# A state-space mixer with a routed expert layer: x projected once, lag tables multiplied on TensorE, powers from coarse and fine factors

## The reference

```python
xz = jnp.einsum('bld,ed->bel', hidden_states, W_in)
x, z = jnp.split(xz, 2, axis=1)
xp = jnp.pad(x, ((0, 0), (0, 0), (w - 1, 0)))          # w = 4 taps, one filter per channel
x = lax.conv_general_dilated(xp, conv_w[:, None, :], (1,), 'VALID', ...)
x = jax.nn.silu(x + conv_b[None, :, None])
# the state-space kernel: dt = exp(log_dt), A = -exp(log_A_real) + i A_imag
# Ct = (C_re + i C_im) * (exp(dt A) - 1) / A
k = 2.0 * jnp.einsum('hn,hnl->hl', Ct, jnp.exp(dtA[:, :, None] * t)).real
y = causal_convolution(x, k)                           # by FFT in the reference
y = (y + x * D[None, :, None]) * jax.nn.silu(z)
mixed = jnp.einsum('bhl,dh->bld', y, W_out)
x = layernorm(hidden_states + mixed)
# each token goes to the one of 8 experts with the largest logit
y = relu(x @ w1[e] + b1[e]) @ w2[e] + b2[e]
out = layernorm(x + y)
```

## Time and profile before

| what | value |
|---|---|
| measured time, median of 3 (range) | 266.92 us (265.96 to 268.56) |
| profiled execution: span | 263.8 us |
| TensorE, matmuls busy | 239.2 us (91%) |
| TensorE, weight loads busy (beside the matmuls) | 215.1 us (82%) |
| VectorE busy | 177.0 us (67%) |
| ScalarE busy | 187.1 us (71%) |
| GpSimd busy | 139.8 us (53%) |
| moved by DMA | 52.06 MB, 197 GB/s on average |
| instructions | 8892 |

### The profile page before, as it was taken

The page is one execution under the profiler, slowest core; times in us unless marked ns, Lnnn a source line. Parts: engine busy times, 40 slices in busy tenths (PEclk is TensorE's granted clock), DMA queues, the critical chain, the costliest instruction groups (busy, mean ns, idle before and its releaser), DMA issues.

```text
span 263.8 us, 8892 instructions
## 1 busy us (share of the span) xinstructions
PE 239.2 (91%) x2763; PEld 215.1 (82%) x2764; DVE 177.0 (67%) x552; ACT 187.1 (71%) x528; POOL 139.8 (53%) x208
## 2 busy tenths in 40 slices
PE   8999979999999899999979999359989999999970
PEld 4888768888887678888869999349979999899960
DVE  1889995997218657777724878842877676566672
ACT  2999999856998778888655665207667777667740
POOL 6000000400009989999624687878746656657545
PEclk9999999999999999999999999759999999999995
DMA  7697884600399999999293221647865676677600
GB/s 232 180 313 288 346 334 150 244 0 0 105 310 332 310 279 296 308 320 302 66 361 120 93 93 41 212 92 191 220 179 172 200 210 164 203 195 208 189 34 6
DMA packets 54267, 52.06 MB, mean 197 GB/s; under 512 B 4415, under 2 KB 42817, under 8 KB 54114
## 3 DMA queue, kind: packets, MB, share of 16 engines
q1 hardware_dynamic: 51506, 46.65, 59.2%
q0 software_dynamic: 2304, 4.34, 4.6%
q10 hardware_dynamic: 432, 0.79, 0.8%
HBM read 38.14 MB, written 14.07 MB: 198 GB/s over the span
## 4 chain that ended last, share of the span: by engine, by line
PE 59%; DVE 10%; ACT 10%; POOL 9%; issue 6%; DMA 5%; SPq 1%; DVEq 0%; ACTq 0%; POOLq 0%
PE banks L1292 13%; PE banks L1477 9%; PE banks L1487 8%; PE banks L1370 7%; POOL dispatched_rows L568 5%; ACT BR L672 5%; PE banks L1380 5%; PE banks L1384 4%; PE banks L1275 3%; PE banks L1357 3%; PE banks L1435 2%; DMA X<-dispatched_rows 2%; POOL RE L558 1%; DMA out<-X 1%; POOL out L576 1%
## 5 line engine op out<-in xcount | busy, mean ns | idle before, releaser
L515 POOL TENSOR_TENSOR Wx<-BR,RE 128x384 f32 (+1 forms) x32 | 47.9, 1548 | 27.9 <-PE banks L1292 26.6
L1292 PE MATMUL banks<-Wx,XT 128*128 128x256 f32 x256 | 59.9, 380 | 1.7 <-ACT Z L643 1.7
L809 ACT ACTIVATE Z<-banks,BR 128x128 f32<-128x128 f32 x156 | 44.6, 368 | 18.4 <-PE banks L1477 18.3
L1292 PEld LDWEIGHTS banks<-Wx,XT 128*128 128x128 f32 x256 | 48.4, 190 | 9.0 <-issue 2.2
L576 POOL DMA_INDIRECT out<-X x39 | 38.4, 986 | 27.8 <-DVE X L1233 15.3
L1477 PE MATMUL banks<-Z 128*128 128x128 f32 x312 | 42.7, 281 | 0.4 <-ACT Z L798 0.2
L1487 PE MATMUL banks<-BR,Z 128*128 x312 | 41.1, 276 | 1.2 <-DVE X L1216 1.2
L1477 PEld LDWEIGHTS banks<-Z 128*128 128x128 f32 x312 | 39.0, 196 | 1.0 <-issue 0.5
L1487 PEld LDWEIGHTS banks<-BR,Z 128*128 128x128 f32 x312 | 37.8, 192 | 1.5 <-issue 1.5
L568 POOL DMA_INDIRECT dispatched_rows<-TR,CR x32 | 31.0, 970 | 9.3 <-POOL RE L558 9.3
L1057 DVE TENSOR_TENSOR X<-banks,Z 128x256 f32 (+1 forms) x32 | 20.4, 636 | 9.1 <-PE banks L1384 9.1
(11 more groups left out here) (220 smaller groups left out, 469.6 us busy)
## 6 DMA issues: line engine op xcount, KB each, us to landing
TR<-kernel_rows SPq DMA_DIRECT2D x32, 512.0 KB, 6.5
Z<-w SPq DMA_DIRECT2D x39, 256.0 KB, 3.1
dispatched_rows<-TR SPq DMA_DIRECT2D x3, 2310.0 KB, 8.8
X<-dispatched_rows SPq DMA_DIRECT2D x39, 66.0 KB, 2.1
XT<-hidden_t SPq DMA_DIRECT2D x10, 256.0 KB, 3.1
RE<-decay_and_turns SPq DMA_DIRECT2D x2, 1024.0 KB, 7.4
BR<-w SPq DMA_DIRECT2D x1, 2048.0 KB, 8.2
dispatched_rows<-TR SPq DMA_DIRECT2D x1, 1848.0 KB, 7.8
```

The costliest lines, as they stand in the source:

```text
L515: nc.gpsimd.tensor_tensor(BC[:, k, 0:LAGS, :].rearrange("p m (s r n) -> p (m s) r n", s=STRIPS, r=2), Btab[:, :, :, :, :, one].rearrange(" ...
L809: last = nc.scalar.activation(HT[:, j, c * P:c * P + P], bank[UP_BANKS[j]][:, c * P:c * P + P], ACT.Relu, bias=B1[:, bass.ds(experts[j] * ...
L1292: last = mm(bank[X_BANKS[k]][:, j * CHAN:(j + 1) * CHAN], XT[:, slot, at:at + CHUNK], Wx[:, tap, :], start=(tap == 0), stop=(tap == TAPS - 1))
```

## The change

- **x.** The input features are projected once, for two batches and 128 channels at a time, as channels by positions (`project_x`, L1208 of the new code, matmuls of 512 columns; eight steps of two). The taps are added afterwards: ScalarE writes the last tap with the bias (`last_tap`, L706), VectorE adds the other three from PSUM (`add_taps`, L948), TensorE transposes the result (`turn_x`, L1225) and ScalarE stores it (`keep_x`, L713). The gates are projected as before (`project_gates`, L1215), and pass through Silu as they are stored (`keep_z`, L719), so the group loop has no Silu of gates.
- **Powers.** Sines, cosines and exponentials are computed for 28 angles per state (16 fine steps, 8 coarse ones, 3 lags, one half step), 896 columns (L691 to L694, L917 to L921), multiplied (L930). The exponential table of 128 positions is the product of coarse and fine powers (`expand`, L345): for each half of the groups VectorE forms the first product, GpSimd the second, VectorE adds them (L959). `Sel` and the coefficients are now made by GpSimd (L523 to L567). The table is in descending order of position and has 128 positions instead of 129.
- **Lag tables.** GpSimd writes small turning matrices (`Rot`, L571), TensorE multiplies the exponential table with them (`state_tables`, L1238): 14 rounds, 128 matmuls with 32 rows of weights and 96 columns, two row strips by turns, into banks 6 and 7, each round copied by ScalarE to `Btab` (`keep_states`, L726). `group_tables` on GpSimd is a copy (L583).
- **Order.** TensorE projects and sums in the order shown below. SyncE no longer waits for the filling transfers before the Toeplitz loads, and loads the output weights at the start. `X` and `Z` are laid out as tiles by channels. The parameters come as `channels` (taps, bias, skip weight) and `states` (with the real and imaginary coefficients swapped on the odd rows).

```diff
-        X = sb("X", [P, CHAN, TILES])
-        Z = sb("Z", [P, CHAN, TILES])
+        X = sb("X", [P, TILES, CHAN])
+        Z = sb("Z", [P, TILES, CHAN])
...
+        def expand(engine, out, part, by_coarse, by_fine):
+            count = part.stop - part.start
+            shape = [P, count, COARSE, FINE]
+            return engine.tensor_tensor(
+                out.rearrange("p g (b a) -> p g b a", b=COARSE), by_coarse[:, part, :].unsqueeze(3).to_broadcast(shape),
+                by_fine[:, part, 0:FINE].unsqueeze(2).to_broadcast(shape), ALU.mult)
...
+                sp.wait_ge(s_x, (b - A_BATCH) // 2 * 2 + 2)
+                sp.wait_ge(s_zp, b - A_BATCH + 1)
+                load_batch(sp, b)
+
+            sp.wait_ge(s_kx, 2)
...
-            sp.wait_ge(s_fill, 16 * len(FILLS))
...
+            pool.wait_ge(s_exp1, 1)
+            tt(v(EA_SQ), v(EA), v(EA), ALU.mult)
+            done(tt(v(AI_SQ), prm[:, A_IM, :], prm[:, A_IM, :], ALU.mult))
+            done(tt(v(DEN), v(EA_SQ), v(AI_SQ), ALU.add))
...
+            for part in (slice(0, GROUPS // 2), slice(GROUPS // 2, GROUPS)):
+                count = GROUPS // 2 * LAGS * 2
+                tt(Rot[:, part, :].rearrange("p g (m c) -> p (g m) c", c=FINE),
+                   turned[:, part, :, :].rearrange("p g m r -> p (g m r)").unsqueeze(2).to_broadcast([P, count, FINE]),
+                   same_state[:, :].unsqueeze(1).to_broadcast([P, count, FINE]), ALU.mult).then_inc(s_rot, 1)
+
+
+            pool.wait_ge(s_far, 1)
+            for part in halves:
+                expand(nc.gpsimd, products[:, part, :], part, second_coarse, sine).then_inc(s_second, 1)
...
-                one = bass.ds(g, 1)
-                falls = decay.rearrange("p m (s n g) -> p (m s) n g", s=STRIPS, g=GROUPS)[:, :, :, one].rearrange("p m n g -> p m (n g)")
-                nc.gpsimd.tensor_tensor(
-                    BC[:, k, 0:LAGS, :].rearrange("p m (s r n) -> p (m s) r n", s=STRIPS, r=2),
-                    Btab[:, :, :, :, :, one].rearrange("p m s r n g -> p (m s) r (n g)"),
-                    falls.unsqueeze(2).to_broadcast([P, LAGS * STRIPS, 2, PAIR * STATES]), ALU.mult).then_inc(s_bc, 1)
-
+                nc.gpsimd.tensor_copy(BC[:, k, 0:LAGS * P],
+                                      Btab[:, bass.ds(g, 1), :, :].rearrange("p g s c -> p (g s c)")).then_inc(s_bc, 1)
+
+            pool.wait_ge(s_rot, 2)
             pool.wait_ge(s_c, 2)
...
+            def last_tap(i):
+                j = i % 2
+                act.wait_ge(s_x, i + 1)
+                wait_past(act, s_xtr, i - 1)
+                nc.scalar.activation(xc[:, i % 2, :, :], pair_banks(i % 2 * 2), ACT.Identity,
+                                     scale=channel[:, j, TAPS - 1:TAPS], bias=channel[:, j, TAPS:TAPS + 1]).then_inc(s_x3, 1)
+
+            def keep_x(i):
+                j, b = i % 2, i // 2 * 2
+                act.wait_ge(s_xtr, i + 1)
+                for k in range(2):
+                    last = nc.scalar.activation(x_tiles[:, b + k, :, j * P:(j + 1) * P],
+                                                bank[4 + k][:, :].rearrange("p (k c) -> p k c", k=CHUNKS), ACT.Copy)
+                last.then_inc(s_xe, 1)
+
+            def keep_z(b):
+                act.wait_ge(s_zp, b + 1)
+                nc.scalar.activation(z_tiles[:, b, :, :],
+                                     banks[:, 6 * 512:8 * 512].rearrange("p (k c) -> p k c", k=CHUNKS), ACT.Silu).then_inc(s_z, 1)
+
+            def keep_states(h):
+                at, half = h // 2 * ROUND, h % 2
+                count = min(ROUND, GROUPS - at)
+                act.wait_ge(s_b, h + 1)
+                nc.scalar.activation(Btab[:, at:at + count, half * 2:half * 2 + 2, :].rearrange("p g s c -> p s g c"),
+                                     pair_banks(6)[:, :, 0:count * LAGS * STRIP].rearrange("p s (g c) -> p s g c", g=count),
+                                     ACT.Copy).then_inc(s_bt, 1)
...
+            for b in range(3, BATCH):
+                keep_z(b)
+            keep_x(2)
+            last_tap(4)
+            for h in range(0, 3):
+                keep_states(h)
...
-            def gate_silu(r):
-
-
-                part = Z[:, bass.ds(r * 2 * GH, 2 * GH), :].rearrange("p c t -> p (c t)")
-                nc.scalar.activation(part, part, ACT.Silu).then_inc(s_zs, 1)
...
+            for at, table in ((1, sine), (2, cosine)):
+                dve.wait_ge(s_sin, at)
+                tt(table[:, :, 0:DECAYED], table[:, :, 0:DECAYED], fall[:, :, 0:DECAYED], ALU.mult).then_inc(s_dwn, 1)
...
+            def add_taps(i):
+                j, slot = i % 2, i % 2
+                dve.wait_ge(s_x3, i + 1)
+                for back in range(1, TAPS):
+                    if back > 1:
+                        dve.wait_ge(s_xk, i * LAGS + back - 1)
+                    stt(xc[:, slot, :, back:], pair_banks(i)[:, :, 0:SEQ - back], channel[:, j, TAPS - 1 - back:TAPS - back],
+                        xc[:, slot, :, back:], ALU.mult, ALU.add).then_inc(s_xk, 1)
+
+            dve.wait_ge(s_ch, 16)
+            add_taps(0)
+            add_taps(1)
+            for half, part in enumerate(halves):
+                expand(nc.vector, Etab[:, part, :], part, first_coarse, cosine).then_inc(s_vstep, 1)
+                steps[0] += 1
+                dve.wait_ge(s_vstep, steps[0])
+                dve.wait_ge(s_second, half + 1)
+                tt(Etab[:, part, :], Etab[:, part, :], products[:, part, :], ALU.add).then_inc(s_c, 1)
+            add_taps(2)
...
+                tt(X[:, :, cols], bank[4 + k][:, 0:GH * TILES].rearrange("p (h t) -> p t h", h=GH), Z[:, :, cols], ALU.mult)\
+                    .then_inc(s_yc, 1)
...
+            def project_x(i):
+                j = i % 2
+                wait_past(pe, s_xk, (i - 1) * LAGS)
+                for k in range(2):
+                    b = i // 2 * 2 + k
+                    pe.wait_ge(s_xt[b % A_BATCH], (b // A_BATCH + 1) * 16)
+                    last = mm(bank[i % 2 * 2 + k][:, :], Win[:, j * P:(j + 1) * P], XT[:, b % A_BATCH, :], start=True, stop=True)
+                last.then_inc(s_x, 1)
+
+            def project_gates(b):
+                pe.wait_ge(s_xt[b % A_BATCH], (b // A_BATCH + 1) * 16)
+                wait_past(pe, s_z, b)
+                for k in range(CHUNKS):
+                    last = mm(bank[6 + k // 2][:, k % 2 * CHAN:(k % 2 + 1) * CHAN], XT[:, b % A_BATCH, k * P:(k + 1) * P],
+                              Win[:, CHAN:], start=True, stop=True)
+                last.then_inc(s_zp, 1)
+
+            def turn_x(i):
+                pe.wait_ge(s_xk, (i + 1) * LAGS)
+                wait_past(pe, s_xe, i)
+                for k in range(2):
+                    for chunk in range(CHUNKS):
+                        at = slice(chunk * P, (chunk + 1) * P)
+                        last = nc.tensor.transpose(bank[4 + k][:, at], xc[:, i % 2, k, at], ident[:, :])
+                last.then_inc(s_xtr, 1)
+
+            def state_tables(h):
+                at, half = h // 2 * ROUND, h % 2
+                count = min(ROUND, GROUPS - at)
+                if h == 0:
+                    pe.wait_ge(s_kx, 1)
+                wait_past(pe, s_bt, h)
+                pe.wait_ge(s_rot, 1 if at + count <= GROUPS // 2 else 2)
+                for g in range(count):
+                    for k in range(2):
+                        rows = slice((half * 2 + k) * STRIP, (half * 2 + k + 1) * STRIP)
+                        last = mm(bank[6 + k][:, g * LAGS * STRIP:(g + 1) * LAGS * STRIP], Etab[rows, at + g, :], Rot[rows, at + g, :],
+                                  start=True, stop=True)
+                last.then_inc(s_b, 1)
...
+            turn_x(2)
+            project_x(4)
+            for h in range(0, 3):
+                state_tables(h)
+            turn_x(3)
+            project_x(5)
+            for h in range(3, 6):
+                state_tables(h)
...
+            pe.wait_ge(s_xe, PAIRS)
+            pe.wait_ge(s_bt, HALF_ROUNDS)
```

709 lines of the change are left out of this document (282 added, 427 removed).

## The result

The changed kernel takes 283.88 us (median of 4 runs, 283.35 to 284.36), the kernel before 267.74 (265.96 to 268.57) on the same chip: 1.062 times as long (95% interval 1.057 to 1.067), 16 us slower. The forecast was 277, 10 us slower, with a range of 263 to 290. The ratios in this document are of runs within 1.5% of the fastest of their kernel.

The account below looks back on a forecast made before the run. TensorE was taken to bound the kernel. Table at 50.0, plus 41.5 and 2.0 to the first group, plus 47.3 for groups ends at 140.8 against 130.3: 266.9 + 10.5 = 277.4, said as 277 us, range 263 to 290.

Parts of the forecast that it names:

- The table: First half of the preparation: exponential table whole at 50.0 us, after GpSimd's coefficients, matrices and products and VectorE's sums.
- the strided row taken down: GpSimd's two-input price, 3.5 ns an element divided by 1.57: 2.2 ns, so 3.6 us a matrix product, 4.7 a table product.
- The turn-taking: While the table is made, VectorE and GpSimd do not run such work side by side; VectorE's sum waits for GpSimd until 43.1.
- rival 1: Engines hardly hold each other, or GpSimd is fast: table whole at 39.3, first group at 81, total 265; chance 0.26.
- the second half: From whole table to first group, on TensorE's order: 41.5 us plus 2.0 for the clock, first group at 93.5.
- the waits for ScalarE: Between lag-table rounds: copies 11.7 us less 4.5 beside transposes, hops 1.7, ScalarE's other work 1.0.
- 2 us more: Start of the second half: after 8 us of idling TensorE's clock is 0.50, so its first work takes twice as long.
- rival 4: Clock stays at the lower level through the lag-table rounds: up to 12 us more, total 289; chance 0.05.
- The groups: Stage of 32 groups: TensorE's 47.0 us unchanged plus 0.3 of stalls, 47.3 us, ending at 140.8.
- The 3 us that I gave back: Group stage: of 3.3 us of stalls all but 0.3 vanish, since the tables from DRAM are ahead.
- The rest: Last stage, after the groups: only the layout of `X` read by its transposes changes, so it stays at 133.5 us.
- Rival 2: Row strips do not load side by side in lag-table rounds: 2.2 us a round, 14 us more, total 291; chance 0.12.

Follow-up runs that it names:

- e1: Changed kernel with VectorE forming both products of the exponential table and GpSimd none: 283.55 us, 1.060 times the kernel before.
- e11: Changed kernel with Toeplitz loads of groups 9 to 32 bringing only four of eight channels: median 281.84 us, runs from 278.5 to 287.3.
- e2: Changed kernel with each lag-table round's ten matmuls ordered one row strip after the other instead of by turns: 303.47 us, 1.137 times the kernel before.
- e3: Changed kernel with nine unread 512-column matmuls added where TensorE waits for ScalarE's copy of a lag-table round: 271.80 us, 1.017 times the kernel before.
- e4: Changed kernel with lag-table rounds using two pairs of banks by turns instead of one: 273.78 us, 1.023 times the kernel before.
- e9: e7 with bank pairs of the last two lag-table blocks swapped and kernel rows behind seven gates instead of eight: 262.44 us, 0.979 times the kernel before.
- e10: e9 with five unread 512-column matmuls: two after the last gates, one before the last transposes, two before the groups; 261.35 us, 0.974 times the kernel before.
- e8: e7 with both products of the exponential table on VectorE: 264.98 us, 0.994 times the kernel before.
- e7: Changed kernel with two bank pairs each for gates and rounds, turning matrices after the table, third taps between VectorE's product and sum: 264.11 us, ratio 0.985.
- e5: Changed kernel with both products on VectorE and unread matmuls filling TensorE's waits between rounds: 270.65 us, 1.012 times the kernel before.

## Why the prediction was right, and where not

The direction, the size within its range, and the order of the work came out; the sum hides errors of both signs.

- **The table.** Forecast 50.0, measured 42.7, 7.3 us earlier. GpSimd's coefficients were done at 21.15 instead of 24.2: operations of 32 elements that VectorE did not hold took 0.25 us, the lower end of what I took. GpSimd's products took 3.66 us (1.8 ns an element) and the matrices 2.8, where I had 4.7 and 3.6 from the strided row taken down; that term was 3.7 us too large. Some 0.5 us are left over.
- **The turn-taking** was right, and exactly as the earlier trace rows had let it be seen. In the changed kernel:

```profile
32.35 3.67 POOL L345 TENSOR_TENSOR BR<-BR 128x2048 f32<-128x2048 f32 x1
32.49 5.67 DVE L959 TENSOR_TENSOR CR<-CR,BR 128x2048 f32<-128x2048 f32 x1 [6.39 <-POOL BR L345]
```

  VectorE's sum, 2.29 us elsewhere, came 0.14 us behind GpSimd's instruction and lasted until 38.1, 2.1 us past its end at 36.0. In the same way GpSimd's second matrix waited for VectorE's product (4.85 us instead of 2.81). Operations with an input from PSUM (L948, 1.28 us each) were not held. The Trainium skill ("SBUF — State Buffer", "SBUF: two separate sides") says that whichever starts first holds a shared pair of ports for its whole instruction, if VectorE has two inputs in SBUF; these rows agree.
- **GpSimd's product.** The 4497 ns of the Trainium skill ("GPSIMD Engine Reference", "Performance versus the Vector engine"), weighed in the prediction, are too high for this form: 3.66 us. VectorE's 2.29 agrees with its 2293.
- **A second limit that I had not priced.** The kernel rows also wait for the last gates, which go through one pair of banks with ScalarE's Silu between: 3.17 us a batch, done at 43.25:

```profile
40.23 1.97 PE L1215 MATMUL banks<-Win,XT 128*128 128x256 f32 x8 [1.21 <-ACT Z L719]
43.31 1.95 PE L1266 MATMUL banks<-CR,TR 128*32 128x128 f32 x64 [1.11 <-ACT Z L719]
```

  The prediction itself had the last gates at about 42 and yet let rival 1 start the second half at 39.3. That rival (265) would therefore not have come out even with a fast GpSimd; in e1, with the table at 39.9, the kernel rows began at 42.4 and the time stayed.
- **The second half.** Forecast 41.5 + 2.0 for table to first group, measured 51.8. Rounds of 1.31 us instead of 1.1 are some 2.5 us of it; the waits for ScalarE, what is left of the 51.8, are 9.5 us, where I had 9.9. The step "2 us more" for the clock is the one that failed: 8.5 us. I had let it be low once, behind the idle time before the third transposes. It fell instead between rounds, three times up to the groups, though TensorE was busy for 73% of 48 to 52 us, just before the first fall. This was the price of rival 4 (up to 12 us, chance 0.05), which I held far too unlikely; the clock did not stay down, as that rival had it, but went down and up. That the total still came within 7 us of the forecast is in part luck: the table came 7.3 us too early and hid this.
- **The groups.** Forecast 47.3, measured 53.0. The lower clock in the first two is 2.4 us. The 3 us that I gave back "as the tables are ahead" are still there: they were not waits for tables (e11). Nor were they all stalls: in the groups of the kernel before, TensorE's waits in the profile are only

```profile
PE banks L1370 <- issue: 1.2, 2, 1.0
```

  of the 3.3 us by which that stage is longer than 32 times 1.47.
- **The rest**: 133.5, measured 134.2.
- **Rival 2** (row strips not side by side) was refuted by e2: 0.20 us alone, 0.13 in pairs. (The kernel rows, from which the prediction took its case of strips side by side, are 32 matmuls in 64 records, as it has them; the text on the kernel before calls the records matmuls.)

Of the 16 us, then, the clock is 10 to 11 (e3: 12.1 less with it held, part of that by shorter stalls). That the rest is TensorE's row of rounds and copies is argued from the sum; e4, which shortens it, changes the clock as well. Undoing GpSimd's part alone changes nothing (e1). Two bank pairs, a shorter first half and fewer waits make the same plan 2.1% faster than the kernel before (e9), with five unused matmuls on top 2.6% (e10).

## What to carry to other kernels

Busy time taken from the bounding engine is worth little where the engine then waits for others at each step: 41 us of matmuls left, and each small round that waits about 1 us for another engine's copy costs its wait, and can cost the clock on the work behind it. Before splitting work between two engines, look in the trace for whether they hold each other: here GpSimd and VectorE took turns, so the split gave no time (e1) and about 1 us at most (e8). And price a second chain to the same point (here the gates), or a gain on the first is cut off there.

## What the runs showed of the hardware that I had not expected

- Added matmuls made the kernel 12.1 us faster (e3); the granted clock stayed at 1.00 with them. Where TensorE waited 1.07 us between rounds, it went to 0.50 near 52, 66 and 90 us; from 74 to 89, with the same waits, it stayed up.
- The first fall, at 52 to 54 us, came in kernels with different work just ahead of it (the changed kernel, e1, e2, e4, e7, e8), in e7 after 10 us (43 to 53) in which TensorE was busy for 9.4. In e9 it came at 47. In e3, e5 and e10 it did not come; e10's only fillers ahead of it stood at 35 and 38 us. Why it falls there is not shown.
- Matmuls of 32 rows run in pairs of row strips at 0.13 us each and strip by strip at 0.20 (e2); two rounds in a row, of two different pairs, at 0.105 (e4, 2.11 us for 20).
- VectorE's additions and products of 2048 elements from SBUF waited for GpSimd's running instruction (5.67 and 3.83 us instead of 2.29); its taps with one input in PSUM did not, 1.3 us each with and without it.
